# Attention loop: at a block's first step, the first weighing and the second scores change places on TensorE

## The chip, the cores and the metric

One core of a Trainium2 chip runs the whole kernel, one launch. The metric is the device time in microseconds; the median of three runs of the kernel before is 2947.93 us.

## The reference

Input x has 2 x 1024 tokens of 128 values. Four stages are added to it one after the other, each on a layer norm of x: a state-space scan, a mixture of eight experts, an attention stack, and a feed-forward with 4-bit rounding. The change lies in the attention stack, six layers of this kind:

```python
q = (h @ wq.T + bq).reshape(bh, sl, 16, 8)
k = (h @ wk.T + bk).reshape(bh, sl, 16, 8)
scores = jnp.einsum('blhd,bmhd->bhlm', q, k) * inv_sqrt_d
w_avg = jax.nn.softmax(scores, axis=-1).mean(axis=1)      # mean over the heads
new_w = jax.nn.softmax(w_avg + rel[None], axis=-1)
sa = jnp.einsum('blm,bme->ble', new_w, h)
h1 = ln(h + sa); h2 = ln(h1)
out = ln(h2 + relu(h2 @ w1.T + b1) @ w2.T + b2)
```

So two softmaxes follow each other: one per head over 1024 keys, then one over their mean plus a term of the distance.

## The kernel before, in words

The attention part is one software pipeline over six layers, two sequences and all tokens. Its unit is a **score tile** x: 32 query rows times four heads on the 128 partitions, times 1024 keys. There are N = 1536 tiles. Four tiles (all 16 heads) belong to the same 32 queries, eight tiles make a **block** (64 queries), two blocks a tile of 128 queries, eight blocks a **half** (512 queries, half of one sequence in one layer). There are 192 blocks and 24 halves.

What happens to tile x, and where:

- TensorE, `scores(x)` (L706 to L721): eight matmuls, 512 columns each, into `bank[x % 3]`. It waits for `exp >= x - 2`, that is, for the exponential of tile x-3, which read the same bank last.
- VectorE, `rowmax(x)` (L1286 to L1292): the negated maximum of each row into NM.
- ScalarE, `soft(x)` (L976 to L984): the exponential with that bias, into buffer `x % 9` of E, with the sum of the row. For x >= 9 it waits for `weigh >= x - 8`, that is, for the weighing of tile x-9, which read the same buffer last.
- VectorE, the reciprocals RZ (L1302), once in four tiles, and POOL, `diag` (L1551): four diagonal matrices dg out of them.
- TensorE, `weigh(x)` (L723 to L732): eight matmuls (four in the code) that divide by the row sums and add up over the heads, into bank 6. The first weighing of a group of four waits for dg, and the first of a block (x a multiple of eight) also for `evac`, since bank 6 has to be read out before it is written again.
- ScalarE, the evacuation `evac` (L941 to L945): the exponential of the block's mean, bank 6 into acc. POOL multiplies by the distance term (L1492), VectorE turns it over (L1233), and TensorE's attend pieces (L663) make the second weighting. Layer norms, the feed-forward (ff1, L675; its relu on ScalarE, L956; ff2, L682) and the projections for the next layer (L691, L700) follow as **post pieces**.

The order on each engine is written out by hand. A step q handles two tiles on each engine. On ScalarE it is soft(2q), soft(2q+1), each followed by the pieces of its place (a, b); the evacuation of block b comes after soft(2q+1) of step q = 4b + 7. On VectorE it is rowmax(2q+1), the reciprocals, pieces m, rowmax(2q+2), pieces e. On TensorE it is what the change touches: scores 2q+3, pieces of place g, weigh(2q-6), scores 2q+4, pieces of place h, weigh(2q-5). 2q-6 is a multiple of eight at q = 4b + 7, the **fresh** steps in what follows, one per block. There ScalarE evacuates block b while TensorE is to begin block b+1 in the same bank.

The tables `HALF_DUE` (L162) and `END_DUE` (L178, the last half) say at which step of a half a post piece falls due, and at which place. Counted in the eight blocks of a half, the fresh step has at place g: in the first block the transposes `pjt` (L691), in the fourth `ff1_00 ff1_01 ff1_10` (each waits for ScalarE), in the fifth `ff1_30 ff1_31`, in the sixth `ff2_4 ff2_5`, in the second, third, seventh and eighth nothing. The relu `re3` (L956) stands on ScalarE one step behind the fresh step of the fifth block, after its second exponential, and `ff2_0 ff2_1` wait for it at place h of the same step. The attend pieces of 128 queries fall at place g of the step ahead of every second fresh one. The first half has no post work of a half before it.

Of the kernel before, what the change touches and what calls it, by code (L numbers as in the profile page):

```python
# [214 lines left out]
def last(engine, step, place):  # L215

    return LAST[engine].get((step - 1 - PAIRS, place), "").split()
# [19 lines left out]
def due(engine, step, place):  # L237

    out = []
    step -= 1  # L240
    for half in range(max(-2, step // 32 - 3), min(HALF_N, step // 32 + 1)):
        places = END_DUE if half == HALF_N - 1 else HALF_DUE
        for p in places[engine].get((step - 32 * half - 31, place), "").split():
            if p[:2] in ("pj", "sp"):
                if half < HALF_N - 4:
                    out.append((half, p))
            elif p == "fin":
                if half >= HALF_N - 4:
                    out.append((half, p))
            elif half >= 0:  # L250
                out.append((half, p))
    for tile in range(max(0, step // 8 - 2), min(TILES, step // 8 + 1)):
        for p in TILE_DUE[engine].get((step - 8 * tile - 7, place), "").split():
            out.append((tile, p))
    for block in range(max(0, step // 4 - 2), min(BLOCKS, step // 4 + 1)):
        for p in BLOCK_DUE[engine].get((step - 4 * block - 3, place), "").split():
            out.append((block, p))
    return out
# [46 lines left out]
def build(nc, io):  # L305
    ctx = ExitStack()
    with ctx:
# [8 lines left out]
        def pb(i):  # L316
            return bank[i // 2][:, (i % 2) * 512:(i % 2) * 512 + 512]
# [142 lines left out]
        def unit(half):  # L460

            return half // 4, half // 2 % 2, half % 2, half // 2
# [240 lines left out]
        def attention_pe(e):  # L703
            e.wait_ge(s["mask"], 4)

            def scores(x):  # L706
                group, hq = divmod(x, 4)
                half, r0 = group // 16, group % 16 * 32
                l, b, hf, u = unit(half)
                if x % 128 == 0:  # L710
                    e.wait_ge(s[f"stackk{b}0"], 144 * (l + 1))
                    e.wait_ge(s[f"stackk{b}1"], 144 * (l + 1))
                if x % 64 == 0:
                    e.wait_ge(s[f"stackq{b}{hf}"], 144 * (l + 1))
                if x >= 3:
                    e.wait_ge(s["exp"], x - 2)
                for k in range(2):
                    for i in range(4):
                        inst = PE_.matmul(bank[x % 3][32 * i:32 * i + 32, k * 512:k * 512 + 512], QS[:, half % 2, 4 * hq + i, r0:r0 + 32],  # L719
                                          KS[:, b, 4 * hq + i, k * 512:k * 512 + 512], start=True, stop=True)  # L720
                inst.then_inc(s["scores"], 1)  # L721

            def weigh(x):  # L723
                block, grp, hq = x // 8, x // 4 % 2, x % 4
                if x % 4 == 0:
                    e.wait_ge(s["diag"], x // 4 + 1)
                if x % 8 == 0 and block:
                    e.wait_ge(s["evac"], block)
                for k in range(4):
                    inst = PE_.matmul(pb(6)[32 * k:32 * k + 32, 256 * grp:256 * grp + 256], dg[:, x // 4 % 3, x % 4, :],  # L730
                                      E[:, x % NE, :].rearrange("p (i k c) -> p k i c", k=4, c=32)[:, k], start=(hq == 0), stop=(hq == 3), skip_group_check=True)
                inst.then_inc(s["weigh"], 1)  # L732

            for x in range(3):
                scores(x)
            for q in range(STEPS):
                old = 0 <= q - 3 < PAIRS
                if 2 * q + 3 < N:
                    scores(2 * q + 3)
                for n, p in due("PE", q, "g"):  # L740
                    post_pe(e, n, p)
                if old:
                    weigh(2 * q - 6)
                if 2 * q + 4 < N:
                    scores(2 * q + 4)
                for p in last("PE", q, "g"):
                    ffn_pe(e, p)
                for n, p in due("PE", q, "h"):
                    post_pe(e, n, p)
                if old:  # L750
                    weigh(2 * q - 5)
                for p in last("PE", q, "h"):
                    ffn_pe(e, p)
# [54 lines left out]
        def tensor(e):  # L808
            scan_pe(e)
            fence_pe(e, 1)  # L810
            experts_pe(e)
            fence_pe(e, 2)
            attention_pe(e)
# [952 lines left out]
```

## Time and profile before

| what | value |
|---|---|
| median of three runs (2945.22, 2947.93, 2948.14) | 2947.93 us |
| profiled execution: span; its own time is not given apart | 2950.1 us |
| busy over the span: TensorE, VectorE, ScalarE, POOL | 87%, 85%, 80%, 47% |
| weight loads on TensorE, beside its matmuls | 47% |
| mean granted TensorE clock | 0.962 of full |
| attention, first scores to last row maximum | 624.8 to about 2818 us |

Times in the rows below are microseconds; a row of the timeline gives the start from the span's beginning, the duration (from the first start to the last end where several instructions are merged), engine, line, operation, the tiles written and read, and in brackets how long the engine had been idle before it and who released it. A matmul's end is modelled and overlaps the next one's start: groups that follow each other 0.43 us apart are shown with 0.61 us each. "issue" as a releaser is idle time for which the profile shows no wait. The profiler took one execution.

### The profile page before, as it was taken

How to read it: one execution, taken by the hardware profiler on the slowest of the kernel's cores; microseconds unless marked ns; L12 is line 12 of the kernel's file. 1: busy time of each engine (PE TensorE's matmuls, PEld its weight loads, DVE VectorE, ACT ScalarE, POOL GpSimd, SP SyncE). 2: the span in 40 equal slices, each digit the busy share in tenths (PEclk: the TensorE clock that was granted, in tenths of full speed). 3: DMA queues.
4: the chain of work that ended last, by engine and by line, in shares of the span. 5: the costliest groups of instructions: out<-in, count | busy, mean ns of one | idle time of the engine just before them, and what ended most of it. 6: DMA issues, size and time to landing. Idle time of an engine off the chain costs nothing.

```text
span 2950.1 us, 78807 instructions
## 1 busy us (share of the span) xinstructions
PE 2555.2 (87%) x30925; PEld 1398.7 (47%) x30925; DVE 2520.5 (85%) x3657; ACT 2358.2 (80%) x4175; POOL 1389.7 (47%) x2752
## 2 busy tenths in 40 slices
PE   6877799978998899989999899899899988898856
PEld 3444476744444444444445444444454444444435
DVE  4888736389999989999999999999999989899966
ACT  5887443459999889888999999899989989899832
POOL 3443412112465534655445654455644456344564
PEclk8888899989999999999999999999999999999978
DMA  2000000322222123131331222322213212230000
GB/s 63 1 1 1 16 1 12 60 46 45 39 34 43 26 38 58 30 44 18 45 60 31 43 33 30 60 36 38 38 25 60 41 32 37 25 45 10 2 1 15
DMA packets 86770, 94.44 MB, mean 32 GB/s; under 512 B 4592, under 2 KB 84736, under 8 KB 85632
## 3 DMA queue, kind: packets, MB, share of 16 engines
q1 hardware_dynamic: 86400, 89.41, 19.2%
q8 instruction: 244, 4.00, 0.6%
q14 instruction: 126, 1.03, 0.2%
HBM read 69.47 MB, written 19.92 MB: 30 GB/s over the span
## 4 chain that ended last, share of the span: by engine, by line
PE 44%; DVE 22%; issue 17%; ACT 10%; POOL 6%; DVEq 0%; DMA 0%; ACTq 0%; POOLq 0%
DVE NM L1292 14%; PE bank L730 11%; PE bank L719 10%; ACT E L983 5%; PE bank L645 4%; PE bank L635 4%; PE bank L663 3%; PE bank L675 3%; PE bank L555 2%; PE bank L682 2%; PE bank L572 2%; POOL acc L1492 1%; DVE ET L1233 1%; DVE hs L1113 1%; ACT dBT L886 1%
## 5 line engine op out<-in xcount | busy, mean ns | idle before, releaser
L1292 DVE TENSOR_REDUCE NM<-bank 128x1 f32<-128x1024 f32 x1536 | 1800.6, 1208 | 130.7 <-PE bank L719 117.9
L983 ACT ACTIVATE E<-bank,NM 128x1024 f32<-128x1024 f32 x1536 | 1709.4, 1116 | 228.0 <-DVE NM L1292 170.5
L730 PE MATMUL bank<-E,dg 128*32 128x256 f32 x12288 | 967.8, 384 | 100.1 <-ACT acc L945 88.3
L719 PE MATMUL bank<-KS,QS 128*32 128x512 bf16 x12288 | 966.2, 384 | 100.5 <-ACT E L983 69.4
L1551 POOL TENSOR_TENSOR dg<-mask,RZ 128x128 f32<-128x128 f32 x384 | 153.2, 399 | 923.9 <-DVE RZ L1302 806.2
L730 PEld LDWEIGHTS bank<-E,dg 128*32 128x32 f32 x12288 | 360.2, 110 | 431.9 <-issue 222.1
L719 PEld LDWEIGHTS bank<-KS,QS 128*32 128x32 bf16 x12288 | 311.6, 96 | 532.3 <-ACT E L983 358.3
L983 ACT ACTIVATION_READ_ACCUMULATOR E<-bank,NM 128x1 f32 x1536 | 304.8, 198 | 0.0
L1492 POOL TENSOR_TENSOR acc<-acc,rel 128x256 f32<-128x256 f32 x384 | 272.6, 731 | 10.6 <-ACT acc L945 10.6
L663 PE MATMUL bank<-H,ET 128*128 128x129 f32 x1536 | 201.2, 284 | 10.5 <-DVE ET L1233 6.3
L663 PEld LDWEIGHTS bank<-H,ET 128*128 128x128 f32 x1536 | 182.6, 194 | 51.9 <-issue 42.6
L1221 DVE SCALAR_TENSOR_TENSOR EO<-bank,OH,EO 128x128 f32<-128x128 f32 x256 | 72.0, 344 | 136.0 <-PE bank L645 135.8
L931 ACT ACTIVATE HS<-bank,cst 128x512 f32<-128x512 f32 x128 | 87.3, 686 | 118.7 <-PE bank L635 118.7
L1233 DVE STREAM_TRANSPOSE ET<-acc 128x512 f32<-128x512 f32 x192 | 135.0, 703 | 16.8 <-POOL acc L1492 16.5
L555 PE MATMUL bank<-ident,dBT 128*128 128x128 f32 x512 | 92.9, 313 | 53.5 <-DVE hs L1113 41.7
L645 PEld LDWEIGHTS bank<-W,HS 128*128 128x128 f32 x1024 | 124.2, 192 | 30.4 <-issue 29.7
L675 PE MATMUL bank<-hT,WL 128*64 128x256 f32 x768 | 110.7, 398 | 25.3 <-ACT UB L956 21.5
L555 PEld LDWEIGHTS bank<-ident,dBT 128*128 128x128 f32 x512 | 69.0, 161 | 118.5 <-issue 67.6
L645 PE MATMUL bank<-W,HS 128*128 128x128 f32 x1024 | 124.6, 275 | 0.0
L635 PE MATMUL bank<-RTr,W 128*128 128x512 f32 x256 | 123.3, 605 | 0.1
L886 ACT ACTIVATE dBT<-UT,BT 128x256 f32<-128x256 f32 x256 | 108.6, 496 | 16.8 <-PE bank L555 16.4
L945 ACT ACTIVATE acc<-bank 128x512 f32<-128x512 f32 x192 | 113.3, 590 | 6.0 <-PE bank L730 6.0
(230 smaller groups left out, 2834.9 us busy)
## 6 DMA issues: line engine op xcount, KB each, us to landing
KS<-scratch SPq DMA_DIRECT2D x216, 128.0 KB
QS<-scratch SPq DMA_DIRECT2D x216, 128.0 KB
scratch<-UB SPq DMA_DIRECT2D x24, 768.0 KB, 3.7
WL<-in_wl SPq DMA_DIRECT2D x6, 1091.0 KB, 18.7
X<-in_x SPq DMA_DIRECT2D x4, 256.0 KB, 6.1
W<-in_moe_w SPq DMA_DIRECT2D x1, 1024.0 KB, 8.4
out<-X SPq DMA_DIRECT2D x8, 128.0 KB, 1.8
rel<-in_rel SPq DMA_DIRECT2D x1, 960.0 KB, 4.7
```

What stands on the lines that cost most here:

```text
L555: inst = PE_.transpose(pb(4 + n % 2)[:, t * 128:t * 128 + 128], dBT[:, g % 2, t, c * 128:c * 128 + 128], ident[:, :])
L635: PE_.matmul(pb(2 * (n % 2) + hc), W1[:, ex, hc * 128:hc * 128 + 128], RTr[:, toks(j)], start=True, stop=True).then_inc(s["moe_up"], 1)
L645: inst = PE_.matmul(pb(4 + q % 2)[:, t * 128:t * 128 + 128], HS[:, q % 3, hc, t * 128:t * 128 + 128], W2[:, ex, hc, :], start=(hc == 0), s ...
L663: inst = PE_.matmul(o[:, 0:129], ET[:, i, :], H[:, n // 8 % 3, i, :], start=(i == 0), stop=(i == 7))
L675: inst = PE_.matmul(o[64 * i:64 * i + 64, w], wl(l, "w1", fc * 128 + 64 * i, 64), hT[:, w], start=True, stop=True)
L719: inst = PE_.matmul(bank[x % 3][32 * i:32 * i + 32, k * 512:k * 512 + 512], QS[:, half % 2, 4 * hq + i, r0:r0 + 32], KS[:, b, 4 * hq + i, ...
L730: inst = PE_.matmul(pb(6)[32 * k:32 * k + 32, 256 * grp:256 * grp + 256], dg[:, x // 4 % 3, x % 4, :], E[:, x % NE, :].rearrange("p (i k c ...
L983: A_.activation(E[:, x % NE, :], bank[x % 3][:, :], ACT.Exp, bias=NM[:, x % 4:x % 4 + 1], accum_out=ZS[:, quad % 3, j:j + 1]).then_inc(s[" ...
L1233: V.transpose(ET[:, :, 64 * j:64 * j + 64].rearrange("p i (g q) -> p g i q", g=2), acc[:, n % 2, :].rearrange("p (g i q) -> p g i q", g=2, ...
L1292: V.tensor_reduce(NM[:, x % 4:x % 4 + 1], bank[x % 3][:, :], AX.X, ALU.max, negate=True).then_inc(s["rowmax"], 1)
L1492: G.tensor_tensor(y, y, rel_of(n % 16 * 64 + 32 * grp), ALU.mult).then_inc(s["rel"], 1)
L1551: G.tensor_tensor(dg[:, quad % 3, :, :], mask[:, :].unsqueeze(1).to_broadcast([128, 4, 32]), RZ[:, quad % 3, :].unsqueeze(2).to_broadcast( ...
```

## The change

At a fresh step the weighing of the new block's first tile is issued behind the scores of tile 2q+4 and no longer ahead of them. At all other steps, and on all other engines, nothing changes; no instruction is added or removed.

```diff
                 for n, p in due("PE", q, "g"):
                     post_pe(e, n, p)
-                if old:
+                fresh = (2 * q - 6) % 8 == 0
+                if old and not fresh:
                     weigh(2 * q - 6)
                 if 2 * q + 4 < N:
                     scores(2 * q + 4)
+                if old and fresh:
+                    weigh(2 * q - 6)
                 for p in last("PE", q, "g"):
                     ffn_pe(e, p)
                 for n, p in due("PE", q, "h"):
```

## Rows read from the trace of the kernel before

**Rows 1.** Stretch 740 to 2800 us: length, then busy time of each engine, clock, DMA.

```profile
740.00:2800.00 2060.00, 1853.00 (x26406) 959.71 (x26399) 1908.99 (x2462) 1850.86 (x3238) 1078.24 (x2318) 0.99 0.24 37
```

The columns are TensorE, its weight loads, VectorE, ScalarE and POOL.

**Rows 2.** Groups of instructions, same stretch: busy us, mean ns | idle us before, releasers.

```profile
L1292 DVE TENSOR_REDUCE NM<-bank 128x1 f32<-128x1024 f32 x1439 | 1687.5, 1208 | 122.7 <-PE bank L719 110.6
L983 ACT ACTIVATE E<-bank,NM 128x1024 f32<-128x1024 f32 x1439 | 1601.5, 1116 | 198.1 <-DVE NM L1292 142.6 <-PE bank L730 44.6 <-issue 0.2
```

**Rows 3.** Waits, same stretch: who waited for whom: us, times, longest us.

```profile
PE bank L730 <- ACT acc L945: 79.1, 92, 1.1
...
ACT E L983 <- PE bank L730: 44.6, 51, 6.9
```

**Rows 4.** Timeline of VectorE, fourth block of two halves that follow each other.

```profile
1502.23 1.22 DVE L1292 TENSOR_REDUCE NM<-bank 128x1 f32<-128x1024 f32 x1 [2.15 <-PE bank L719]
...
1592.17 1.23 DVE L1292 TENSOR_REDUCE NM<-bank 128x1 f32<-128x1024 f32 x1 [2.15 <-PE bank L719]
```

**Rows 5.** Timeline, fresh step of a third block, no piece at g.

```profile
1578.12 0.59 ACT L945 ACTIVATE acc<-bank 128x512 f32<-128x512 f32 x1
...
1578.85 0.64 PE L730 MATMUL bank<-E,dg 128*32 128x256 f32 x8 [0.67 <-ACT acc L945]
...
1579.96 1.22 DVE L1292 TENSOR_REDUCE NM<-bank 128x1 f32<-128x1024 f32 x1
```

**Rows 6.** Timeline, a fresh step of the first half.

```profile
657.12 1.12 ACT L983 ACTIVATE E<-bank,NM 128x1024 f32<-128x1024 f32 x1
...
658.96 0.64 PE L730 MATMUL bank<-E,dg 128*32 128x256 f32 x8 [1.06 <-ACT acc L945]
...
659.39 0.64 PE L719 MATMUL bank<-KS,QS 128*32 128x512 bf16 x8
...
660.07 2.36 DVE L1292 TENSOR_REDUCE NM<-bank 128x1 f32<-128x1024 f32 x2 [0.67 <-PE bank L719]
```

**Rows 7.** Timeline: scores that waited for an exponential.

```profile
1537.46 1.11 ACT L983 ACTIVATE E<-bank,NM 128x1024 f32<-128x1024 f32 x1 [0.18 <-DVE NM L1292]
...
1538.72 0.61 PE L719 MATMUL bank<-KS,QS 128*32 128x512 bf16 x8 [0.34 <-ACT E L983]
```

**Rows 8.** Timeline, fresh step of a fifth block and what follows.

```profile
1513.17 0.64 PE L730 MATMUL bank<-E,dg 128*32 128x256 f32 x8
1513.63 0.61 PE L719 MATMUL bank<-KS,QS 128*32 128x512 bf16 x8
...
1513.94 1.12 ACT L983 ACTIVATE E<-bank,NM 128x1024 f32<-128x1024 f32 x1
...
1514.28 2.35 DVE L1292 TENSOR_REDUCE NM<-bank 128x1 f32<-128x1024 f32 x2 [0.44 <-PE bank L719]
...
1515.04 0.68 ACT L956 ACTIVATE UB<-bank,WL 128x512 f32<-128x512 f32 x1
...
1515.90 0.49 PE L682 MATMUL bank<-WL,UB 128*128 128x128 f32 x2
```

**Rows 9.** Timeline, fresh step of a sixth block, then the group behind the attend pieces.

```profile
1523.76 0.64 PE L730 MATMUL bank<-E,dg 128*32 128x256 f32 x8
...
1524.21 0.61 PE L719 MATMUL bank<-KS,QS 128*32 128x512 bf16 x8
...
1524.53 1.12 ACT L983 ACTIVATE E<-bank,NM 128x1024 f32<-128x1024 f32 x1
...
1524.87 2.35 DVE L1292 TENSOR_REDUCE NM<-bank 128x1 f32<-128x1024 f32 x2 [0.51 <-PE bank L719]
...
1525.94 0.61 PE L719 MATMUL bank<-KS,QS 128*32 128x512 bf16 x8
...
1532.74 0.61 PE L719 MATMUL bank<-KS,QS 128*32 128x512 bf16 x8
...
1533.70 1.21 DVE L1292 TENSOR_REDUCE NM<-bank 128x1 f32<-128x1024 f32 x1
```

**Rows 10.** Timeline of TensorE: one of its isolated stalls.

```profile
2514.67 0.64 PE L730 MATMUL bank<-E,dg 128*32 128x256 f32 x2 [4.81 <-issue]
```

## The prediction

> **What bounds the kernel now.** I read the stretches first: from 740 to 2800 us, all of it attention, VectorE is busy 1909 of 2060 us, TensorE 1853, ScalarE 1851 [rows 1]. Three engines are near full, so no change of order can give more than the idle time that is left, and that has to be idle time of the engine that sets the pace just there. Second, the groups of instructions: of VectorE's some 151 idle us, 123 lie before the row maxima (L1292), 111 of them released by the scores (L719); ScalarE has 198 idle us before its exponentials (L983), most of it behind VectorE [rows 2]. Third, the waits: the weighing (L730) waited 92 times for the evacuation of the accumulating bank (L945), 79 us in all. That is the wait on which the change acts. But the table has the opposite wait too: 51 times an exponential waited for a weighing, 45 us, the longest 6.9 us [rows 3]. E has nine buffers, so the exponential of tile x needs the weighing of x-9. Last I read the timeline at the fresh steps. There are 192 of them, 24 half-sequences (halves) of eight blocks, and the pattern repeats: the same 2.15 us idle stands at 1502.23 and at 1592.17, 89.9 us apart [rows 4].
>
> **The change part by part.** It adds and removes no instruction and no DMA. At a fresh step TensorE's queue was: scores 2q+3, any post pieces of place g, weighing W of the block's first tile, scores S of 2q+4. Now S stands ahead of W. Both groups take about 0.43 to 0.45 us of issue, so whatever stands behind the pair has its old place, unless a wait differs. S gets earlier, by 0.45 us where TensorE was busy, by more where it stood waiting for L945. W gets later by 0.45 us, except where L945 released it.
>
> (a) *Blocks with no post piece at g* (second, third, seventh and eighth of a half). At 1578.85 W starts 0.14 us after L945 ends, after 0.67 us of idle TensorE. S, which needs only the exponential before L945, fits into this idle time, and W stays where it is. Yet the row maximum at 1579.96 has no idle time before it: VectorE is itself late there [rows 5]. Value: 0. The evacuation frees TensorE, not the engine that sets the pace.
>
> (b) *The first half*, in which no post work exists yet. W waits 1.06 us, S starts at 659.39, and the row maximum starts at 660.07 after 0.67 us idle [rows 6]. The exponential that S needs began at 657.12 and took 1.12; the lag from an exponential to the scores that wait for it is 0.15 us (1537.46 + 1.11 to 1538.72) [rows 7], so S can start at 658.39, 1.0 us earlier, and the 0.67 us go. I count that once per two blocks, the blocks between having much less, so 4 x 0.67 = 2.7, and with the few such places in later halves **-3 us**. Ends: 0 and -5.4, if every one of the eight had it.
>
> (c) *The fourth block of a half* (ff1 pieces at g, each waiting for ScalarE). VectorE idles 2.15 us before the row maximum at 1502.23 [rows 4], the largest gap in the half. S comes 0.45 us earlier, but the next scores keep their place behind the pair and VectorE then waits for those. Value 0; ends -0.45 x 22 = -10 and 0.
>
> (d) *The fifth block.* W at 1513.17 runs to S at 1513.63, and the row maximum at 1514.28 had 0.44 us idle. This can shrink. But the exponential at 1513.94 comes 0.77 us after W's start, just as the one at 1524.53 does after the W at 1523.76, and that one has the same tile distance, nine: W is what they run directly behind, with no slack [rows 8, 9]. With W at 1513.62 the exponential starts 0.4 to 0.45 us later. Behind it in ScalarE's order stands the relu (L956, 1515.04, 0.68 us), and behind that, on TensorE, ff2 (L682) at 1515.90, 0.18 us after the relu's end [rows 8]. So the delay comes back to TensorE. Part of the 0.18 us may have been TensorE's own, so I take 0.28 to 0.45, mostly 0.35 us for everything behind.
>
> (e) *The sixth block.* TensorE arrives 0.35 us late, S gains 0.45: the scores of 1524.21 start at 1524.11, and of the 0.51 us idle before 1524.87 only 0.1 goes. W is late by 0.35 + 0.45 = 0.80 us, so the exponential of 1524.53 starts at 1525.33 and ends at 1526.45. The scores at 1525.94 need exactly this one; with the lag of 0.15 they start at 1526.60, **0.66 us late** (0.53 with the smaller term of (d)). From there TensorE works through ff2, the three tiles and the attend pieces without a pause, so the scores at 1532.74 go to 1533.27 to 1533.40. A row maximum starts 0.66 us after its scores at the earliest (1524.21 to 1524.87), that is at 1533.93 to 1534.06, where it was at 1533.70 [rows 9]. VectorE's slack of 0.30 us takes the rest. I take **+0.25 us** a half, the lower part of 0.23 to 0.36, as later small gaps can take some of it; 22 halves have these pieces in this form: **+5.5 us**. Ends: +0.65 x 22 = +14, if no slack absorbs it; -(0.44 + 0.51) x 22 = -21, if W's delay never reached TensorE and both gaps closed.
>
> (f) *The first block* (transposes at g): W is late by a few tenths with more slack; 0, ends +-1. POOL's and SP's queues are untouched; the evacuation itself isn't later by its own inputs. (g) TensorE has isolated stalls that the profile calls issue, like 4.81 us at 2514.67 [rows 10]. They may fall elsewhere; 0, ends +-5.
>
> Sum: -3 + 5.5 = +2.5 us. It is made against the profiled execution, 2950.1 us of span, its own time not being given apart; that is 2.2 us above the median of 2947.93, and I put the difference on the median: **2950.4 us**. A measurement of this kernel can tell about 0.2%, 5.9 us, from no change.
>
> **A rule against my reading.** By the rows, VectorE has the highest occupancy and a gap at just the place where S comes earlier [rows 1, 2]. The Trainium skill, in "Perfetto Trace Analysis", sections Identifying the Most-Contended Engine and Optimization Strategy, says to take the engine of the highest occupancy, to judge TensorE by its weight loads and not by matmul time, and to make the dependencies start sooner that cause that engine's gaps. By that rule this change is right and its gain is rival A's. The rows of (d) and (e) say otherwise: in those blocks the order of TensorE's queue sets the gaps.
>
> **The rivals.** *A, faster:* the late weighing is absorbed by ScalarE, which has 198 idle us [rows 2]; then both gaps close and (b) comes on top: -21 - 3 = -24, 2924 us; with half of the delay absorbed about 2937. For it: every gap of ScalarE before later exponentials of the block. Against: the relu that ff2 waits for stands before the largest of those gaps. Chance 0.20.
>
> *B, slower:* one mechanism, E's nine buffers. W behind S delays the exponential nine tiles on, it delays the scores three further on, and TensorE hands the delay through the attend pieces. It decides where the scores of 1532.74 are late by more than VectorE's 0.30 us of slack there. Its price is 0.40 to 0.65 us a half: +9 to +14 less 3, that is +6 to +11, 2954 to 2959 us. Chance 0.36; my own step (e) is its small form.
>
> *C, no effect:* in the blocks where L945 is waited for only TensorE's idle time is moved, and the other blocks cancel. The diff does swap as it says (2q-6 is a multiple of eight at every fourth step), so a change that doesn't act has 0.02; it would leave 2948.
>
> **How the numbers follow.** Forecast 0.42, and C's 0.02, are within 0.2%: 0.44. A 0.20 is faster, B 0.36 slower. The forecast's own range is 2944 to 2956. For 8 in 10 the range takes in B whole with the stalls' 5 us, to 2962, and A down to half of its gain, 2936.
>
> **What the profile will show.** Right: the waits of L730 for L945 shrink from 92 times and 79 us to well under half (scores now fill them); the waits of L983 for L730 rise from 45 us to some 60 or more; the idle time before L1292 falls by 10 to 25 us in the fifth and sixth blocks, and comes back later in the half; the half stays at 89.9 us, give or take 0.4. In the first half the 0.67 us before every second fresh row maximum are gone. Wrong, toward A: L983 waits no more for L730 than before and a half takes 89.3 us or less. Wrong, toward B: a half takes 90.4 us or more, and the scores behind the attend pieces of the sixth block release a row maximum that they did not release before.

## The result, and the profile after

The changed kernel takes 2933.89 us (median of 19 runs, 2918.93 to 2942.09), the kernel before 2941.04 us in the 19 runs beside it (2928.86 to 2953.10). The ratio is **0.9971, with an interval of 0.9959 to 0.9983**: 8.5 us faster by the ratio, 5.0 to 12.1; the two medians lie 7.2 us apart. The forecast was no change that can be told, with 2.5 us on the slow side.

The profiled execution of the changed kernel spans 2917.1 us, 33 us less than that of before. Most of this is chance: its own time, 2918.93 us, is the lowest of the 19 runs. One execution of each must not be compared as a whole; what repeats in every half can.

Line numbers are three higher from the change on: the row maximum is L1295, the exponential L986, the evacuation L948, the relu L959; scores and weighings keep L719 and L730.

The groups of instructions of the changed kernel from 740 to 2770 us (busy us, mean ns | idle us before, releasers), which answer to [rows 2]:

```profile
L1295 DVE TENSOR_REDUCE NM<-bank 128x1 f32<-128x1024 f32 x1440 | 1691.6, 1207 | 93.8 <-PE bank L719 79.8
L986 ACT ACTIVATE E<-bank,NM 128x1024 f32<-128x1024 f32 x1440 | 1601.6, 1116 | 171.9 <-DVE NM L1295 103.1 <-PE bank L730 55.7 <-issue 5.5
L719 PE MATMUL bank<-KS,QS 128*32 128x512 bf16 x11512 | 887.6, 382 | 128.8 <-ACT E L986 85.7 <-issue 1.6
L730 PE MATMUL bank<-E,dg 128*32 128x256 f32 x11512 | 862.8, 382 | 1.3 <-issue 1.0
```

The wait of the weighings for the evacuation, 79.1 us in 92 waits before [rows 3], is no longer there. VectorE's idle time before the row maxima is 93.8 us where it was 122.7, and ScalarE waits longer for weighings, 55.7 us where it was 44.6. So the swap does what its words say, and part of the idle time that it removes comes back elsewhere. How much of it is the swap's, these rows can't say, as there is a second difference between the two executions: TensorE's idle time without a wait. The waits of the kernel before, 740 to 2760 us (us, times, longest us):

```profile
PEld bank L730 <- issue: 202.0, 298, 5.3
...
PE bank L730 <- issue: 10.1, 4, 4.8
...
PE bank L719 <- issue: 6.6, 3, 2.6
PE bank L663 <- issue: 4.2, 1, 4.2
...
PE bank L675 <- issue: 1.9, 1, 1.9
```

Nine matmul groups waited 22.8 us for nothing that the profile shows; the 4.81 us of [rows 10] is one of them. In the changed kernel's execution there are three, with 2.8 us. This is the term that the prediction put at zero.

The fresh steps themselves. Timeline of the changed kernel, fifth block of the half that [rows 8] show (there it stands 14.08 us later on the time axis):

```profile
1499.09 0.62 PE L719 MATMUL bank<-KS,QS 128*32 128x512 bf16 x8
...
1499.53 1.04 PE L730 MATMUL bank<-E,dg 128*32 128x256 f32 x16
...
1499.76 3.67 DVE L1295 TENSOR_REDUCE NM<-bank 128x1 f32<-128x1024 f32 x3
...
1500.28 1.11 ACT L986 ACTIVATE E<-bank,NM 128x1024 f32<-128x1024 f32 x1 [0.49 <-PE bank L730]
...
1501.38 0.68 ACT L959 ACTIVATE UB<-bank,WL 128x512 f32<-128x512 f32 x1
...
1502.20 1.02 PE L682 MATMUL bank<-WL,UB 128*128 128x128 f32 x7
```

The sixth block, and behind its last "..." the group behind the attend pieces [rows 9]:

```profile
1510.03 0.62 PE L719 MATMUL bank<-KS,QS 128*32 128x512 bf16 x8
...
1510.47 1.03 PE L730 MATMUL bank<-E,dg 128*32 128x256 f32 x16
...
1510.70 2.52 DVE L1295 TENSOR_REDUCE NM<-bank 128x1 f32<-128x1024 f32 x2
...
1511.21 1.11 ACT L986 ACTIVATE E<-bank,NM 128x1024 f32<-128x1024 f32 x1 [0.47 <-PE bank L730]
...
1512.47 0.61 PE L719 MATMUL bank<-KS,QS 128*32 128x512 bf16 x8
...
1519.27 0.61 PE L719 MATMUL bank<-KS,QS 128*32 128x512 bf16 x8
...
1519.93 1.23 DVE L1295 TENSOR_REDUCE NM<-bank 128x1 f32<-128x1024 f32 x1
```

Both gaps, 0.44 and 0.51 us, are closed: the row maxima have no idle time before them. But both exponentials now wait for the weighing, 0.49 and 0.47 us. Adding 14.08 us to the rows of the sixth block and comparing with [rows 9]: the scores of 1524.21 come at 1524.11 (0.10 earlier), the exponential of 1524.53 at 1525.29 (0.76 late), the scores of 1525.94 at 1526.55 (0.61 late), those of 1532.74 at 1533.35 (0.61 late), the row maximum of 1533.70 at 1534.01 (0.31 late). Steps (d) and (e) had said 0.10, 0.80, 0.66, 0.53 to 0.66, and 0.23 to 0.36. In the fifth block, too, the exponential, the relu and ff2 come 0.42, 0.42 and 0.38 us later than in [rows 8].

And the half that all this adds up to. Timeline of VectorE in the changed kernel, the largest gap, in the fourth block of two halves seven apart:

```profile
1938.86 1.23 DVE L1295 TENSOR_REDUCE NM<-bank 128x1 f32<-128x1024 f32 x1 [1.70 <-PE bank L719]
...
2568.32 1.23 DVE L1295 TENSOR_REDUCE NM<-bank 128x1 f32<-128x1024 f32 x1 [1.70 <-PE bank L719]
```

629.46 / 7 = 89.92 us, against 89.9 before [rows 4]. The gap itself shrank by 0.45 us and the half did not: most of it stands again before the next row maximum, which had 0.36 us of idle time before the change and has 0.78 us now. The rows that follow 1502.23 and 1938.86, of the kernel before and of the changed one:

```profile
1503.82 2.36 DVE L1292 TENSOR_REDUCE NM<-bank 128x1 f32<-128x1024 f32 x2 [0.36 <-PE bank L719]
```

```profile
1940.87 2.35 DVE L1295 TENSOR_REDUCE NM<-bank 128x1 f32<-128x1024 f32 x2 [0.78 <-PE bank L719]
```

So in the 20 halves of the middle the swap gains nothing, and its gain is at the ends or in the isolated stalls. The first half gains, as step (b) says: from 625 to 740 us VectorE's idle time before row maxima went from 7.4 to 4.6 us. First the rows of the kernel before, then those of the changed one:

```profile
L1292 DVE TENSOR_REDUCE NM<-bank 128x1 f32<-128x1024 f32 x86 | 100.3, 1210 | 7.4 <-PE bank L719 6.6
...
L730 PE MATMUL bank<-E,dg 128*32 128x256 f32 x616 | 49.0, 388 | 6.9 <-ACT acc L945 6.9
```

```profile
L1295 DVE TENSOR_REDUCE NM<-bank 128x1 f32<-128x1024 f32 x88 | 102.8, 1206 | 4.6 <-PE bank L719 3.6
...
L730 PE MATMUL bank<-E,dg 128*32 128x256 f32 x640 | 48.7, 381 | 0.6 <-issue 0.6
```

Measured from the exponential of a half's first tile to that of the next half's, the first half went from 85.5 to 82.8 us, the second from 89.97 to 89.26, and the last stretch, up to the end of the last row maximum, from 92.57 to 91.56. With +0.03 a half for 20 halves, that is -2.7 - 0.7 - 1.0 + 0.6 = **-3.8 us** in this pair of executions. The first half is the uncertain term: in the five executions that keep its old order it takes 84.4 to 88.3 us, in the nine with its new order 81.9 to 84.0. In the two thinned kernels below, where nothing stalls, the same sum is -2.0 us. So **2 to 4 us** of the change lie outside the stalls. The ratio says -8.5. The rest, some 5 us or more, had to be looked for.

### The profile page after: what moved, and what is told of

Same layout as the page of the kernel before. It is cut to its first block, busy times and chain, and to the rows that moved or that the text cites. A ratio compares the mean times of both kernels' runs of the same rounds, so it can differ in the third digit from the quotient of the medians.

```text
span 2917.1 us, 78807 instructions
## 1 busy us (share of the span) xinstructions
PE 2585.8 (89%) x30925; PEld 1342.9 (46%) x30925; DVE 2520.8 (86%) x3657; ACT 2354.9 (81%) x4175; POOL 1388.4 (48%) x2752
## 3 DMA queue, kind: packets, MB, share of 16 engines
q1 hardware_dynamic: 86400, 89.41, 18.8%
## 4 chain that ended last, share of the span: by engine, by line
PE 43%; DVE 20%; issue 15%; POOL 12%; ACT 10%; DVEq 0%; POOLq 0%; DMA 0%; ACTq 0%
DVE NM L1295 13%; PE bank L719 9%; PE bank L730 9%; ACT E L986 5%; PE bank L663 4%; PE bank L645 4%; PE bank L635 4%; PE bank L675 3%; PE bank L682 3%; POOL acc L1495 3%; PE bank L555 2%; PE bank L572 2%; ACT dBT L889 1%; POOL smp L1488 1%; DVE hs L1116 1%
## 5 line engine op out<-in xcount | busy, mean ns | idle before, releaser
L1295 DVE TENSOR_REDUCE NM<-bank 128x1 f32<-128x1024 f32 x1536 | 1803.6, 1207 | 98.3 <-PE bank L719 83.1
L986 ACT ACTIVATE E<-bank,NM 128x1024 f32<-128x1024 f32 x1536 | 1708.2, 1116 | 197.8 <-DVE NM L1295 125.9
L719 PE MATMUL bank<-KS,QS 128*32 128x512 bf16 x12288 | 950.8, 383 | 140.3 <-ACT E L986 94.0
L730 PE MATMUL bank<-E,dg 128*32 128x256 f32 x12288 | 920.6, 382 | 3.4 <-issue 1.7
L719 PEld LDWEIGHTS bank<-KS,QS 128*32 128x32 bf16 x12288 | 258.7, 95 | 662.8 <-ACT E L986 519.1
L730 PEld LDWEIGHTS bank<-E,dg 128*32 128x32 f32 x12288 | 355.2, 109 | 331.2 <-issue 96.5
L986 ACT ACTIVATION_READ_ACCUMULATOR E<-bank,NM 128x1 f32 x1536 | 306.9, 200 | 0.0
L948 ACT ACTIVATE acc<-bank 128x512 f32<-128x512 f32 x192 | 113.6, 592 | 5.1 <-PE bank L730 5.1
```

The costliest lines, as they stand in the source:

```text
L986: A_.activation(E[:, x % NE, :], bank[x % 3][:, :], ACT.Exp, bias=NM[:, x % 4:x % 4 + 1], accum_out=ZS[:, quad % 3, j:j + 1]).then_inc(s[" ...
L1295: V.tensor_reduce(NM[:, x % 4:x % 4 + 1], bank[x % 3][:, :], AX.X, ALU.max, negate=True).then_inc(s["rowmax"], 1)
```

## The experiments

**Method.** Two measures are used. The ratio of the runs to those of the kernel before beside them tells the whole, with an interval of about 5 us either way; differences below are worked out from it unless medians are named. The *undisturbed half* is the distance between the same row maximum in halves that follow each other without an isolated stall; it repeats to 0.04 us and tells only what the order of the work does. Excess is what the third to the twenty-third half of an execution take beyond the undisturbed half, summed.

Eight experiments change only the condition of the swap. Its line, with what each adds:

```diff
-                fresh = (2 * q - 6) % 8 == 0
+                fresh = (2 * q - 6) % 8 == 0 and q < 36                    # e1_first
+                fresh = (2 * q - 6) % 8 == 0 and q >= 36                   # e2_later
+                fresh = (2 * q - 6) % 8 == 0 and q // 4 % 8 in (2, 3, 7, 0)  # e5_noposts
+                fresh = (2 * q - 6) % 8 == 0 and q // 4 % 8 in (1, 4, 5, 6)  # e6_posts
+                fresh = (2 * q - 6) % 8 == 0 and (q < 36 or q // 4 % 8 in (2, 3, 7, 0))  # e9_best
+                fresh = (2 * q - 6) % 8 == 0 and q // 4 % 8 == 5           # e13_fifth
+                fresh = (2 * q - 6) % 8 == 0 and q // 4 % 8 == 6           # e14_sixth
+                fresh = (2 * q - 6) % 8 == 0 and (q < 36 or q // 4 % 8 != 5)  # e15_not_fifth
```

`q // 4 % 8` is the number of the block in its half, with 0 for the eighth.

### Where does the gain lie: the first half or the later ones?

e1_first swaps in the first half alone.

> The swap only at the eight fresh steps of the first half; the other 184 fresh steps keep the old order. Theory 1 (the steady gain of the change is the first half's alone; whatever else the measurement showed comes from fewer or shorter stalls of TensorE behind its instruction loads): the first half takes 82.8 us instead of 85.5, each undisturbed later half 89.9 us, and the time falls by about 3 us, ratio 0.999, with stalls as in the kernel before (eight or so over 1.3 us). Theory 2 (every half gains a little): later halves stay at 89.9 us here too, but the time falls by 1 us at most against some 8 for the whole change.

e2_later swaps in all the others.

> The swap only from the second half on. Theory 1: undisturbed halves take 89.9 us as before, the first half 85.5 us; if the swap itself thins out the stalls, the time still falls by about 5 us (ratio 0.998) with four or so large stalls in place of eight; if the stalls differ by chance alone, the ratio is 1.000. Theory 2: halves of 89.5 us and a ratio of 0.997.

Measured: e1_first 2940.21 us, ratio 0.9981 (0.9963 to 0.9999); its first half takes 82.07 us, the later ones 89.90. e2_later 2938.45 us, ratio 0.9976 (0.9961 to 0.9992); first half 85.53, later ones 89.93. The first half is worth the predicted 3 us. But e2_later gains too, 7 us (2 to 11), though none of its later halves is shorter when nothing disturbs it; only the last stretch gives 1 us. So the swap in the later halves seems to act on what disturbs them.

### The isolated stalls

Each of the nine stalls of TensorE in the profiled execution of before ended 1.3 to 1.9 us after a 16 KB packet of the queue "instruction" had landed, at a time when loads of keys or queries were under way. Not every slow packet stalls TensorE: of the 204 between 740 and 2760 us, 20 took 1.4 us or more, against a median of 1.0, and nine of these belong to the stalls. Transfers of the kernel before from 2509.8 to 2514.7 us, the stretch in which TensorE stood for 4.81 us [rows 10]:

```profile
DMA packets 336, 0.35 MB, mean 71 GB/s; under 512 B 17, under 2 KB 334, under 8 KB 334
...
q1 hardware_dynamic: 334, 0.32, 51.8%
q8 instruction: 1, 0.02, 2.3%
q14 instruction: 1, 0.01, 1.0%
```

One instruction packet among 334 of data, which took half of the time of the 16 DMA engines. Over the whole kernel there are 244 such packets. The theory: a piece of TensorE's program that is fetched during a burst of data comes late, and TensorE runs dry. The test takes the bursts away: from the fifth half on, the loads of keys and queries bring one row of one head, so that scores are made of stale values; everything else, waits and order, stays. It is done to both kernels (the cut below leaves out the index of `scr` and the semaphore at the end).

```diff
+                    m, g = (1, 1) if n >= 4 else (8, 16)
-                    e.dma_start(KS[r0:r0 + 8, b, :, hf * 512:hf * 512 + 512],
-                                scr[...].rearrange("(h d) t -> d h t", d=8))
+                    e.dma_start(KS[r0:r0 + m, b, 0:g, hf * 512:hf * 512 + 512],
+                                scr[...].rearrange("(h d) t -> d h t", d=8)[0:m, 0:g])
```

(and the same for QS.)

> The kernel before, with the loads of K and Q tiles from memory cut to one row and one head each from the fifth half on (attention then works on stale keys and queries; every instruction and wait is kept). Theory 1 (an instruction load that meets the burst of small data packets is late, and TensorE stands still): the stalls of 1.3 to 5 us in the middle of attention vanish, all halves from the fifth to the last but one take 89.9 us, and the time falls by 20 to 30 us to about 2918, with a spread of runs of 3 us at most. Rival (the stalls have nothing to do with the data's traffic): eight stalls as before and about 2941 us.

> The changed kernel with the same cut of the loads. Theory 1: no large stalls either, and the difference to the kernel before with the cut is the first half's alone, 3 us (2915 against 2918). Theory 2 (the swap gains in every half): the difference stays at 7 us or more. If the difference is under 1 us, the first half's gain is given back somewhere.

Measured: e3_before_thin 2913.38 us (2910.00 to 2920.53), ratio 0.9892 (0.9870 to 0.9913); e4_after_thin 2912.92 us (2910.54 to 2914.28), ratio 0.9885 (0.9865 to 0.9905). The kernel before is 31 us faster without the bursts (2944.67 us beside it). The page of e3_before_thin, its DMA slices and queues:

```profile
DMA  2000000412210000000000000000000000000000
...
q1 hardware_dynamic: 38160, 42.58, 5.8%
q8 instruction: 244, 4.00, 0.6%
```

The instruction packets are the same 244, only the data are gone, and with them every isolated stall. Its waits from 740 to 2760 us, then those of e4_after_thin; neither table has a wait of matmuls for "issue":

```profile
DVE NM L1292 <- PE bank L719: 84.0, 111, 2.1
PE bank L730 <- ACT acc L945: 79.1, 92, 1.1
PE bank L719 <- ACT E L983: 62.3, 158, 1.2
...
ACT E L983 <- PE bank L730: 20.3, 46, 0.7
```

```profile
PE bank L719 <- ACT E L986: 85.7, 200, 1.5
...
DVE NM L1295 <- PE bank L719: 75.3, 111, 1.7
ACT E L986 <- PE bank L730: 53.0, 113, 0.7
```

This pair is the cleanest reading of the change, since the stalls are out of both. TensorE's waits for ScalarE fall from 79.1 + 62.3 to 85.7 us; ScalarE's waits for weighings rise from 20.3 us in 46 to 53.0 us in 113; VectorE, the engine that sets the pace, gets 8.7 us of its waits for scores back, but most of it lies elsewhere again: the sum over the whole attention part is the -2.0 us given above. Of the 44.6 us of [rows 3], with a longest wait of 6.9 us, more than half is gone in e3_before_thin: it had been stalls of TensorE seen from ScalarE.

The undisturbed halves of the two kernels, VectorE's timeline eleven halves apart, e3_before_thin and then e4_after_thin:

```profile
1212.14 1.23 DVE L1292 TENSOR_REDUCE NM<-bank 128x1 f32<-128x1024 f32 x1 [2.15 <-PE bank L719]
...
2201.13 1.23 DVE L1292 TENSOR_REDUCE NM<-bank 128x1 f32<-128x1024 f32 x1 [2.15 <-PE bank L719]
```

```profile
765.63 1.23 DVE L1295 TENSOR_REDUCE NM<-bank 128x1 f32<-128x1024 f32 x1 [1.70 <-PE bank L719]
...
1755.18 1.23 DVE L1295 TENSOR_REDUCE NM<-bank 128x1 f32<-128x1024 f32 x1 [1.70 <-PE bank L719]
```

89.91 and 89.96 us: no gain in the middle halves. The medians of the two differ by 0.5 us (five and six runs). So about 31 us of the kernel before are stalls beside the bursts, and the same sum for the changed kernel is 0.9971 x 2944.67 - 2912.92 = 23 us. **The larger part of the change's gain is that its stalls cost less in sum.**

The theory said that TensorE runs dry at the end of a piece of its program, and the traces can be asked for that. TensorE's records of the kernel before are 30925 matmuls, 30925 weight loads and 746 semaphore instructions, 62596 for 244 packets, which is 256.5 each. Counting these records up to the first matmul behind each of the nine stalls gives numbers whose differences are 9, 15, 9, 32, 24, 31, 24 and 9 times 256 exactly. A half has about 2370 of them, so the pattern of the halves doesn't make this so. The same count over the sixteen kept executions with full loads finds 127 such stalls between 740 and 2760 us, and all leave the same remainder by 256: 193 in fourteen executions, 177 in the two of e15_not_fifth and e16_after_third. So the stalls keep step with the packets of the program, as running dry at a packet's border would make them.

A stall has a second price, which the waits don't show: the granted clock of TensorE. The kernel before behind another of its stalls, 4.24 us up to 2418.92; first the stretch from 2420 to 2424 us, where the column before the last two is the clock, then two groups in it:

```profile
2420.00:2424.00 4.00, 4.00 (x32) 2.46 (x35) 1.25 (x4) 1.20 (x2) 0.00 (x0) 0.50 0.00 0
...
2421.59 1.08 PE L730 MATMUL bank<-E,dg 128*32 128x256 f32 x8
2422.44 1.08 PE L719 MATMUL bank<-KS,QS 128*32 128x512 bf16 x8
```

At 0.50, the lower of its two levels (1.2 GHz), the groups follow each other 0.85 us apart, where the rows above have 0.43 to 0.46. Five of the nine stalls of the kernel before have such a stretch, 27.3 us together; the changed kernel's execution has none, nor have the two thinned ones. How much of the 31 us is the clock's and how much the standstill's wasn't measured.

### Blocks with and without post pieces

e5_noposts swaps in the second, third, seventh and eighth block, e6_posts in the other four.

> The swap only in the second, third, seventh and eighth block of each half (no post piece at place g; the evacuation is what the weighing waits for). By the rows so far: undisturbed halves at 89.9 us or a little under, since neither the fifth nor the sixth block loses anything on ScalarE and the gaps of 0.44 and 0.51 us there stay. Theory X (a scores group that fills the wait for the evacuation gives VectorE one tile in hand, and short stalls of TensorE no longer reach it): nearly the whole gain, ratio 0.997, and under 10 us of stalls in the profile where the kernel before has 22.9. Theory Y (the stalls fall where the instruction loads happen to meet the data's bursts): no rule, ratio anywhere in 0.997 to 1.001.

> The swap only in the first, fourth, fifth and sixth block of each half, where post pieces or their waits stand ahead of the weighing. Steady halves: if the late weighing costs what the record's steps (d) and (e) say, 90.15 us or a little more against 89.90, as the part without posts brings nothing; if it is free, 89.8 or less. Theory X: no thinning of the stalls, ratio 1.000 to 1.002. Theory Y: 0.997 to 1.002 by chance.

Measured: e5_noposts 2935.03 us, ratio 0.9977 (0.9961 to 0.9993), e6_posts 2942.29 us, ratio 0.9996 (0.9983 to 1.0009). VectorE's timeline two halves apart, e5_noposts and then e6_posts:

```profile
951.07 1.22 DVE L1295 TENSOR_REDUCE NM<-bank 128x1 f32<-128x1024 f32 x1 [2.15 <-PE bank L719]
...
1130.43 1.23 DVE L1295 TENSOR_REDUCE NM<-bank 128x1 f32<-128x1024 f32 x1 [2.15 <-PE bank L719]
```

```profile
1947.31 1.22 DVE L1295 TENSOR_REDUCE NM<-bank 128x1 f32<-128x1024 f32 x1 [1.70 <-PE bank L719]
...
2127.51 1.23 DVE L1295 TENSOR_REDUCE NM<-bank 128x1 f32<-128x1024 f32 x1 [1.70 <-PE bank L719]
```

179.36 / 2 = 89.68 and 180.20 / 2 = 90.10. Against 89.90, the blocks without post pieces give 0.22 us a half and those with them take 0.20. The two cancel, which is why the full swap shows 89.92. In the halves without a stall two gaps before row maxima are gone in e5_noposts, both too short for the brackets of the timeline: 0.06 us at the fresh step of the eighth block and 0.10 us at that of the first, which this kernel does not even swap. They are most of the 0.22 us.

### Which of the blocks with post pieces costs

> The swap only at the fresh step of each fifth block, where one of the two bursts of data loads falls. By step (d) of the record the late weighing delays TensorE by 0.28 to 0.45 us there, of which VectorE's slack of 0.30 and the gap of 0.44 us take most: undisturbed halves 89.9 to 90.2 us against 89.90. Theory Z1 (the late weighing in the fifth block, just where TensorE runs without a pause, gives the instruction load time to arrive): stalls cost about 7 us less, ratio 0.998 to 1.000 with the steady loss counted in. Rival Z0 (the rarer stalls come from elsewhere or from chance): ratio 1.000 to 1.002.

> The swap only at the fresh step of each sixth block. By step (e) without the delay of (d), the scores there come 0.45 us earlier and the next wait for the late exponential: scores behind the attend pieces late by 0.3 us or so, just VectorE's slack, undisturbed halves 89.8 to 90.1 us. Theory Z1: stalls as in the kernel before, ratio 1.000 +- 0.0015; if this kernel and not the fifth-block one has rarer stalls, Z1 falls.

Measured: e13_fifth 2951.22 us, ratio 1.0014 (0.9999 to 1.0030); e14_sixth 2940.40 us, ratio 0.9987 (0.9970 to 1.0004). Undisturbed halves 90.25 and 89.95 us: +0.35 and +0.05. e13_fifth, VectorE two halves apart:

```profile
947.93 1.23 DVE L1295 TENSOR_REDUCE NM<-bank 128x1 f32<-128x1024 f32 x1 [2.15 <-PE bank L719]
...
1128.43 1.22 DVE L1295 TENSOR_REDUCE NM<-bank 128x1 f32<-128x1024 f32 x1 [2.15 <-PE bank L719]
```

It is the fifth block alone that takes the time back. Its own lateness is the whole of the 0.35; alone, the swap of the sixth adds next to nothing. The first and fourth, by difference, give some: 0.20 - 0.35 - 0.05 = -0.20, if the parts add up. Both medians lie below what the halves make of them: +0.0014 is +4 us where 22 x 0.35 = 7.7, and -0.0013 is -4 us where 22 x 0.05 = +1.1. The intervals are about 5 us either way, so no block can be named as the one that makes stalls cheaper.

### Do the stalls depend on where they fall, or on the order?

A stall falls where the program's place meets a burst. If the gain were only luck in that meeting, moving the whole program by some instructions would undo it. One-column matmuls were put ahead of the attention part, 64 or 32 of them in the code.

```diff
+            for _ in range(64 if k == 1 else 0):      # 32 in e11, e12
+                PE_.matmul(bank[3][0:1, 1023:1024], ident[:, 0:1], ident[:, 0:1], start=True, stop=True)
```

> The kernel before with 64 more one-column matmuls at the first fence, 128 instructions with their weight loads, half of a 16 KB instruction load: all later instruction loads move by half a load against the work. They cost about 2 to 4 us at the fence themselves. Theory Y (the phase of the loads against the bursts decides): once this is taken off, the time differs from the kernel before by several us either way and the large stalls stand in other halves. Theory X: the same 20 us or so of stalls, and the time of before plus the fence's cost.

> The changed kernel with the same 64 matmuls. Theory X: stalls stay under 10 us, and the distance to the kernel before with the shift is again 6 to 9 us. Theory Y: the distance changes to anything between 0 and 15 us, as the phase that the change was timed with is gone. The first half's share of about 3 us stays in any case.

> The kernel before with 32 one-column matmuls at the first fence, a quarter of an instruction load. Theory Y (the phase between instruction loads and data bursts sets the stalls' sum): once 1 to 2 us of fence are off, anything from -8 to +8 us against before. Theory Z (the swap itself makes stalls rarer at any phase): close to the kernel before.

> The changed kernel with the same quarter. Undisturbed halves 89.93 us. Theory Z: again 6 to 12 us below the kernel before with the same shift, as at the two other phases (9 and 14 us). Theory Y: the distance is the 3 us of the undisturbed stretches plus a difference of either sign.

> The changed kernel once more, on the same chip as the others of this set. Ratio 0.997 to 0.998 to the kernel before; the profile shows 89.93 us a half where nothing stalls, and another number of stalls than the first profile's.

The expectations have the size of the move wrong. The trace of e7_before_shift shows each matmul of the code as two, each with a weight load:

```profile
L592 PE MATMUL bank<-ident x128: 163/163/164, 351.5 to 354.6; 128*1 128x1 f32 x128
```

So 64 of them are 256 instructions, one whole packet, and 32 are half a packet. With 64 the borders fall where they fell before: all nine stalls of the kernel before stand in e7_before_shift at the same instructions of the attention part. Only with 32 do they move.

Measured (us; ratio to the kernel before, with its interval; excess over the undisturbed half in the one profiled execution; the last column from the ratios):

| matmuls in the code | old order | new order | new less old |
|---|---|---|---|
| 0 | 2941 to 2946, excess 34.9 | 2933.89, 0.9971 (0.9959 to 0.9983), excess 3.8; again 2934.63, 0.9960 (0.9943 to 0.9977), 18.9 | -8.5, -11.8 |
| 32 | 2944.94, 0.9999 (0.9987 to 1.0010), 19.2 | 2931.71, 0.9956 (0.9941 to 0.9972), 12.1 | -13 |
| 64 | 2953.14, 1.0029 (1.0012 to 1.0045), 26.5 | 2935.75, 0.9982 (0.9964 to 0.9999), 30.0 | -14 |

The new order is faster by 8.5 to 14 us each time (by 9.7 in e16_after_third below), always by more than the 2 to 4 us outside the stalls, and also with the borders moved by half a packet (-13). So the gain is not luck of one place, as far as two places of the borders can tell. Theory Y doesn't explain e7_before_shift: its 8.5 us over the kernel before can't come from a move of the borders, as they stand at the same instructions; up to 3.3 us are the added matmuls themselves (351.4 to 354.6 us), and the rest was not followed up.

Nor did the change put the stalls elsewhere: the eight stalls of e10_after_again stand at eight of the nine borders at which the kernel before stalls, and the three of the changed kernel's first execution at three of them. What differs is their sum, 22.8, 19.9 and 14.1 us of waits in the three executions of the old order against 2.8, 14.1, 9.1 and 22.8 in the four of the new one, and the time at the lower clock, 27.3, 13.7 and 17.1 us against 0, 6.8, 3.4 and 17.1. Single executions scatter too widely (excess 3.8 to 30.0 in the new order) to prove more. The excess of e11_before_shift32 leaves out its first two halves, which took 88.3 and 94.9 us.

### Kernels that should beat both

e9_best keeps the swap in the first half and in the blocks without post pieces.

> The swap at every fresh step of the first half, and after it only in the second, third, seventh and eighth block of each half. The parts so far: undisturbed halves 89.68 us where the kernel before has 89.90 and the changed one 89.93; the first half and the next as in the changed kernel, 4 us less together than before. That adds up to 8 to 9 us less than before and 5 to 6 less than the changed kernel, if stalls are equal. If the late weighing of the posts' blocks is what makes the stalls rarer (theory Z), this kernel lacks it and stands level with the changed one.

e15_not_fifth keeps it everywhere but in the fifth block of the later halves; e16_after_third is the changed kernel once more beside it.

> The swap at every fresh step but those of the fifth blocks after the first half. The fifth block's swap alone lengthened an undisturbed half by 0.35 us and the whole swap left it at 89.93; without it I expect 89.6 us, that is 7 us less over the attention than the changed kernel. If the stalls stay as cheap as in the changed kernel, the ratio is 0.993 to 0.995, better than both kernels; if the relief needed the fifth block too, it is 0.995 to 0.997, level with the changed one.

> The changed kernel once more, on the same chip as the version without the fifth block: ratio 0.996 to 0.9975, undisturbed halves 89.93 us.

Measured: e9_best 2935.00 us, ratio 0.9967 (0.9947 to 0.9987), half 89.67; e15_not_fifth **2928.36 us** (6 runs, 2917.08 to 2934.23), ratio **0.9943 (0.9923 to 0.9962)**; e16_after_third 2933.58 us, ratio 0.9967 (0.9955 to 0.9979). VectorE of e15_not_fifth, five halves apart:

```profile
946.26 1.23 DVE L1295 TENSOR_REDUCE NM<-bank 128x1 f32<-128x1024 f32 x1 [1.70 <-PE bank L719]
...
1394.21 1.23 DVE L1295 TENSOR_REDUCE NM<-bank 128x1 f32<-128x1024 f32 x1 [1.70 <-PE bank L719]
```

447.95 / 5 = 89.59 us, 0.3 less than either kernel. The fifth block thus costs 0.33 us a half on top of all the others, as it cost 0.35 alone, and the first, fourth and sixth together gain 0.08 over e9_best; so the first and fourth do give something, 0.13 us by this count. For 20 halves the 0.3 us are 6 us, and 5.2 us is what its median lies below e16_after_third. Its interval reaches over that of e16, so the step from one to the other rests on the halves more than on the medians. e9_best has the shorter half by 0.25 us too, and yet its median is that of the full swap: in its one profiled execution the excess is 27.0 us, near the upper end of what the new order shows above, so its stalls may have taken the gain; that is not shown.

## Why the prediction was wrong

The forecast was "no change that can be told", the result is faster by 0.29% (0.17 to 0.41). As a ratio, 0.9971 of 2947.93 is 2939.4 us, inside the range of 2936 to 2962; the median of the runs beside it, 2933.89, lies below it.

- **(b), first half: right.** -3 was said; 85.5 to 82.8 us is -2.7 (-1.5 in the thinned pair), and the second half adds -0.7.
- **(d) and (e), fifth and sixth block: right in mechanism and nearly in size.** The chain weighing, exponential, relu, ff2, late scores, late row maximum stands in the rows of after at each of its steps, within 0.05 us of what was said or inside its range. +0.25 us a half was said for the blocks with post pieces, and e6_posts shows +0.20. What the sum hid is its make-up: the fifth costs 0.35 and the sixth alone 0.05, and the first and fourth, put at zero, seem to give 0.13 to 0.2 back, which only differences between kernels show.
- **(a), blocks without post pieces: the step that failed first.** "Value: 0. The evacuation frees TensorE, not the engine that sets the pace" was read from one fresh step [rows 5]. The third block does have no idle time there; the eighth and first do, in gaps of 0.06 and 0.10 us, and e5_noposts shows them at -0.22 us a half, about -4.6 us in 21 halves. A gap of 0.1 us looks like nothing and stands 22 times.
- **(g), isolated stalls at 0 +/- 5: the step that failed most.** They are 31 us of the kernel before, they stand at the borders of the program's packets and go with the bursts of data, and the swap lowers their sum: of 8.5 us gained 2 to 4 lie outside them, and the rest is theirs. The two thin kernels show the part outside alone: -0.5 us in the median, -2.0 in the traces. "They may fall elsewhere" is wrong as well: they kept their places and lost in length.
- **(c) and (f), fourth and first block:** the 2.15 us gap became 1.70 and the half did not shorten in the full kernel, as (c) says for the next scores. Which of the two gives the 0.13 to 0.2 us above was not tried.

The +5.5 us of the later halves came out at +0.6, and the last stretch gave 1.0 us for which the sum had no term. With (a) at -0.22 a half, 21 times, the prediction's own sum of +2.5 would have been -2.1 us. That is still within what counts as no change; without a value for (g) the result could not be reached.

**Of the claims on the profile.** The waits of L730 for the evacuation went not "well under half" but to nothing. The waits of L983 for L730 rose to 55.7 us in the disturbed execution and not to 60; in the thin pair they rose by 33 us. The half stayed at 89.9. The five waits of 0.64 to 0.67 us before row maxima of the first half are gone; one of 0.62 us stands elsewhere.

**The rivals.** Rival A said that both gaps close and nothing returns, a half of 89.3 us or less: the gaps closed and 89.92 came out. The rule to make the dependencies start sooner that the gaps of the most-contended engine wait for, from the Trainium skill, "Perfetto Trace Analysis" (Optimization Strategy), holds here for the blocks in which no engine behind TensorE is late (e5_noposts), and against it stands the fifth block, where filling VectorE's gap of 0.44 us made the half 0.35 us longer. Rival B's mechanism, a late weighing that holds up the exponential nine tiles on, is what the rows of after show, and alone in the fifth block it costs 0.35 us a half (0.40 to 0.65 was said for all), but the other blocks make up for it. A version with ten buffers wasn't tried. Rival C's half without a change in the middle came true by two effects that cancel, which is another thing than no effect.

**What stays open:** why the new order makes the sum of the stalls smaller. In the kernel before they stand 9 to 15 or 62 to 70 us behind a half's start, the second of these about the fresh step of the fifth block; but neither e13_fifth nor e14_sixth can be told from what the halves give, and e5_noposts keeps an excess of 35.4 us. That a stall of the same length costs less in the new order is hardly it: with the borders at the same places, the excess is 1.5 and 1.3 times the waits in the two executions of the old order and 1.3 to 1.4 times in the three of the new one. The waits themselves are shorter in sum, by traces that scatter as said above.

## What to carry to other kernels

When two groups change places in a full queue, follow both: the one moved up fills a gap, and the one moved down is what somebody else waits for; here the gain of some blocks was lost in another, and leaving that one out, where a late relu held TensorE up, was worth 0.3 us a half (2928 against 2934 us). Split a repeating pattern by its places before summing it up as "no change", and count small gaps by how often they stand. Where idle time has no releaser, look at the DMA queues in that stretch before calling it chance: kernels that differ by a few us may differ in nothing but stalls, and one with thinned loads shows what is left. Count the engine's instructions up to each stall: a common divisor of the distances says more than their times do. And count in the trace how many instructions a line of the code becomes before using it as a shift.

## What was not expected of the hardware

- TensorE stood still with nothing to wait for where a 16 KB instruction packet fell among data loads: nine times and 22.8 us in one execution, up to 4.8 us each, 31 us of 2944.67 by the medians. With the same 244 instruction packets and the data cut from 89.41 to 42.58 MB there was none. The nine stand at multiples of 256 instructions of TensorE from each other.
- Five of the nine were followed by a stretch at a granted clock of 0.50, 27.3 us in all, though TensorE had work again.
- These stalls seem to make up most of the scatter between runs: 2928.86 to 2953.10 us for the kernel before in 19 runs, 2910.00 to 2920.53 in the five of e3_before_thin and 2910.54 to 2914.28 in the six of e4_after_thin.
- 64 one-column matmuls ahead of the attention part cost the old order 8.5 us (3.5 to 13 by the interval), though they move the packets' borders by one whole packet only, and 32 cost it nothing that can be told.
